# Row scatters cut into 18 and 28 pieces, each held back to TensorE's pace

## The chip, the cores and the metric

The kernel runs on one core of one Trainium2 chip. A core has TensorE (PE, matrix products), VectorE (DVE), ScalarE (ACT), GpSimd (POOL) and SyncE (SP, which only starts transfers), and 16 DMA engines. Each engine takes its own instructions strictly in order; they meet through semaphores. The metric is device time in microseconds (us) of a whole execution: the median of 3 runs of the kernel before is 1061.18 us (1056.96 to 1062.02). Lower is better.

## The reference, cut to what matters

Two layers work on x of 16 x 256 tokens by 128 values. Layer 0 is gated linear attention and a mixture of 8 experts; layer 1 is causal attention with 16 heads and a mixture of 16 experts. In each, every token goes to its two best experts.

```python
x = L0_attn_x
xn = _layernorm(x)
s = _L0_attn_ref(xn, ...)            # linear attention in chunks of 64, a scan over chunks
g = _silu(_L0_ffn_ref(xn, ...))      # top 2 of 8 experts
x = x + s * g
xn = _layernorm(x)
s = _L1_attn_ref(xn, ...)            # softmax(q k^T / sqrt(8)), causal, 16 heads of 8
g = _silu(_L1_ffn_ref(xn, ...))      # top 2 of 16 experts, tanh * cos(softplus)
return x + s * g
```

The kernel computes only the chosen experts. For this it sorts token rows by expert: every row (its 128 values and one number that says where the result goes) is scattered twice, once for each chosen expert, to a table in device memory (`xs`). The expert stage then reads the table in groups of 512 rows.

## The kernel before, in words

All engines run the same walk (`walk`, L272) over named stages, and each does its own part of a stage. Three stretches matter here.

**Chunks.** `gla(t, part)` is one third of a step of the linear attention. A step t holds work of several batch elements at once: the gates of element t, the decays, queries, keys and values of t-1, the scores of t-2, the states and outputs of t-3, and the normed output of t-4. On GpSimd a step has two small operations: `output_gates(t-4)` in part 0 (a product of 128x256, L1721, from step 4 on), for which DVE's `gated` (L1417) waits, and `chunk_ends(t-1)` in part 1 (a copy of 128x12, L1715), which waits for ACT's exponential (L896). The steps t = 1 to 6 come after `route(0)`, which computes the row numbers, and before the first expert stage. The scan of `decays` on DVE (L1366) marks the steps in a trace.

**The first scatter.** `scatter(0, i, n)` issues 64 indirect transfers from GpSimd (L1685), each of 128 rows, in n pieces. One piece of 6 stands ahead of each of the steps 1 to 6. Then SP loads the first rows of the table (`begin`, `rows`), for which it waits until all 64 have landed, and TensorE turns them (`turn`, L550). TensorE's `turn(0, 0)` stands behind step 6.

**The second attention and the second scatter.** `mha(a, b)` runs eighths a to b-1 of the second attention: each batch element has 8, of which the first six compute scores (`mha1`: L672 to L702) and the last two weigh and turn values (`mha2`: L714, L649). Eighths 32 to 59 run after `route(1)`, four ahead of each `mf(t)`, and beside them stands the second scatter, 64 transfers in 7 pieces. `mf(c)` loads and splits an eighth of the expert weights (ACT L863, DVE L1344); TensorE's first product with them (L586) waits for the last. `turn(1, 0)` again waits for rows that SP loads when all 64 transfers have landed.

GpSimd's transfers wait among themselves only (16 semaphores `rows_moved`, so at most 16 are under way, and every eighth one of the second half also waits for a small table of numbers, L1681). Nothing holds them to TensorE's pace, apart from where `output_gates` and `chunk_ends` stand between them.

Of the kernel before, what the change touches and what calls it, by code (L numbers as in the profile page):

```python
# [51 lines left out]
def build(nc, A, out):  # L52
    with ExitStack() as ctx:
# [7 lines left out]
        def sig(name, per=1):  # L61
            return Sig(ctx.enter_context(nc.semaphore(name)), per)
# [24 lines left out]
        thr, jj, part = cst[:, 664:728], cst[:, 728:808], cst[:, 936:937]  # L87
# [129 lines left out]
        gate2, gate2_ln, decay = sig("gate2", 2), sig("gate2_ln", 4), sig("decay", 3)  # L217
        pn, p_ends = sig("exp_decay", 2), sig("chunk_ends")
        qk, qk_mul = sig("qk", 4), sig("qk_scaled", 4)
        vv, v_moved = sig("v"), sig("v_moved", 2)  # L220
# [24 lines left out]
        m_s2, m_exp = sig("m_s2", 12), sig("m_exp", 12)  # L245
        m_pv, m_pv_act, m_pv_dve = sig("m_pv", 2), sig("m_pv_act"), sig("m_pv_dve")
        m_ot, m_y = sig("m_o_turned", 2), sig("m_y", 4)
# [4 lines left out]
        def last_scatter(l, i):  # L252
            return rows_moved[i].sem, 64 * l + 64
# [18 lines left out]
        def walk(do):  # L272

            def mha(a, b):

                for i in range(a, b):
                    if i % 8 < 6:
                        do["mha1"](i // 8, i % 8 // 2, i % 2 * 2)
                    else:
                        do["mha2"](i // 8, i % 2)  # L280
# [7 lines left out]
                    do["gla"](t, part)  # L288
            do["route"](0)
            for t in range(1, 7):  # L290
                do["scatter"](0, t - 1, 6)
                if t == 1:
                    do["set_later"]()
                for part in range(3):
                    do["gla"](t, part)
                for c in range(8 * (t - 1) // 6, 8 * t // 6):
                    do["w1"](c)
# [14 lines left out]
                    do["norm_end"](g - 2)  # L312
            do["route"](1)
            for t in range(7):
                do["scatter"](1, t, 7)
                mha(32 + 4 * t, 36 + 4 * t)
                do["mf"](t)
            do["mf"](7)
            do["ffn1_begin"]()
# [16 lines left out]
        def _(eng):  # L336
# [447 lines left out]
            def nothing(*_):  # L784
                pass
# [835 lines left out]
        def _(eng):  # L1621
# [39 lines left out]
            def route(l):  # L1661
                eng.wait_ge(*chosen[l].at(1))
                eng.memset(RS[l]["onesc"], 1.0).then_inc(routed_ones.sem, 1)

            def scatter(l, i, n):
                if i == 0:
                    if l == 0:
                        eng.wait_ge(*id_table.at(0))
                    else:
                        for j in range(16):  # L1670
                            eng.wait_ge(*last_scatter(0, j))
                    eng.tensor_copy(xid, idt[:, 0:32]).then_inc(ids_set.sem, 1)
                    eng.wait_ge(*routed[l].at(0, 14))
                    eng.wait_ge(zeroed[l].sem, 16 * (9 + l))
                    eng.wait_ge(*ids_set.at(l, 0))
                for m in range(64 * i // n, 64 * (i + 1) // n):
                    k, t = m // 32, m % 32
                    if k and t % 8 == 0:
                        for j in range(8):
                            eng.wait_ge(rows_moved[(t + j) % 16].sem, 64 * l + 16 * ((t + j) // 16 + 1))  # L1680
                        eng.tensor_copy(xid[:, t:t + 8], idt[:, 32 + t:40 + t]).then_inc(ids_set.sem, 1)  # L1681
                        eng.wait_ge(*ids_set.at(l, 1 + t // 8))
                    if m >= 16 or l:
                        eng.wait_ge(rows_moved[m % 16].sem, 64 * l + 16 * (m // 16))
                    eng.indirect_dma_start(xs[l][:, :], bass.IndirectOffsetOnAxis(ap=slot_i[l][:, m:m + 1], axis=0),  # L1685
                                           xrow[:, t, :], None).then_inc(rows_moved[m % 16].sem, 16)
# [260 lines left out]
```

## Time and profile before

| what | value |
|---|---|
| median of 3 runs | 1061.18 us |
| profiled execution, span from first to last instruction | 1209.8 us |
| mean granted TensorE clock in it | 0.820 |
| TensorE matmuls busy | 865.3 us (72%) |
| DVE, ACT, GpSimd busy | 644.2, 630.8, 461.6 us |
| GpSimd's row scatters (L1685), 128 of them | 126.6 us busy, 989 ns each |

The page gives no other time for the profiled execution than its span, so the span is taken as its own time. It is 148.6 us longer than the median of the runs without a profile. In the rows below a start is in us from the start of the span; "busy" leaves out waiting; in square brackets stands how long the engine sat idle before the row and what ended this. "another core or an unknown queue" and "remote" mean that the profile could not tell what released a wait; there is one core here. "issue" is time for which the profile shows no wait at all.

### The profile page before, as it was taken

Reading aid. Unit: us, or ns where it says so; the run is one execution under the profiler, and the core shown is the slowest. Engines: PE = TensorE matmul, PEld = TensorE weight load, DVE = VectorE, ACT = ScalarE, POOL = GpSimd, SP = SyncE. Lnnn points to the kernel's source line nnn. Section 1 sums busy time; section 2 is a strip of 40 time slices with the busy share of each in tenths; the row PEclk is TensorE's granted clock in tenths of the full one; section 3 lists DMA queues with packets and bytes.
Section 4 is the critical chain, followed back from the end, with each engine's and each line's share of the span. In section 5 each row is a group of like instructions: output and inputs, shape, how many; then the busy total and the mean of one; then the engine's idle time right before and its main releaser. Section 6 shows DMA issues by size and latency. Waiting matters only on the chain.

```text
span 1209.8 us, 23609 instructions
## 1 busy us (share of the span) xinstructions
PE 865.3 (72%) x8916; PEld 647.5 (54%) x8916; DVE 644.2 (53%) x1112; ACT 630.8 (52%) x1095; POOL 461.6 (38%) x486
## 2 busy tenths in 40 slices
PE   5735678989898987079773115989999999998510
PEld 3424566878787876055451003556766766666410
DVE  7663355655555422685575003766576566663345
ACT  5342356665756431255441003668788678876622
POOL 3075450213232344540004771004454455454635
PEclk9676778989898999576695556989999899998855
DMA  9411120000101120600003210210111011110052
GB/s 327 172 55 47 51 59 19 20 27 27 28 28 28 37 55 30 170 1 1 1 1 106 76 52 29 71 54 22 35 32 32 28 36 30 34 29 24 20 148 70
DMA packets 62366, 63.92 MB, mean 53 GB/s; under 512 B 7378, under 2 KB 52322, under 8 KB 62132
## 3 DMA queue, kind: packets, MB, share of 16 engines
q1 hardware_dynamic: 53300, 43.99, 12.5%
q0 software_dynamic: 8960, 18.43, 4.7%
q8 instruction: 77, 1.26, 0.5%
q14 instruction: 29, 0.24, 0.1%
HBM read 31.84 MB, written 30.55 MB: 52 GB/s over the span
## 4 chain that ended last, share of the span: by engine, by line
PE 41%; ACT 17%; issue 13%; DVE 13%; another core or an unknown queue 9%; POOL 4%; DMA 2%; SPq 0%; POOLq 0%; ACTq 0%; DVEq 0%
PE bank L434 4%; ACT L797 4%; PE bank L649 3%; PE bank L586 3%; PE bank L588 3%; POOL ys L1701 2%; PE bank L600 2%; PE bank L702 2%; PE bank L714 2%; PE bank L587 2%; ACT arena L1101 2%; PE bank L462 2%; PE bank L675 2%; PE bank L695 2%
## 5 line engine op out<-in xcount | busy, mean ns | idle before, releaser
L1701 POOL DMA_INDIRECT ys<-arena x152 | 152.4, 1003 | 192.6 <-DVE arena L1463 88.0
L1101 ACT ACTIVATE arena<-bank 128x512 f32<-128x512 f32 x192 | 101.6, 596 | 106.3 <-remote 50.2
L1571 DVE TENSOR_REDUCE arena<-bank 128x2 bf16<-128x512 f32 (+1 forms) x192 | 120.1, 682 | 67.4 <-issue 36.4
L1685 POOL DMA_INDIRECT xs<-arena x128 | 126.6, 989 | 62.2 <-issue 36.2
L586 PE MATMUL bank<-arena 128*128 128x128 bf16 x608 | 134.4, 228 | 11.3 <-DVE arena L1444 10.3
L588 PE MATMUL bank<-arena 128*128 128x128 bf16 x608 | 134.0, 228 | 0.7 <-issue 0.5
L587 PE MATMUL bank<-arena 128*128 128x128 bf16 x608 | 131.5, 223 | 1.1 <-issue 1.1
L797 ACT ACT_TABLE_LOAD x72 | 92.4, 1283 | 1.3
L434 PE MATMUL bank<-arena 128*128 128x256 f32 x256 | 72.0, 441 | 19.2 <-DVE arena L1350 15.8
L1741 POOL TENSOR_TENSOR arena<-arena 128x1024 f32<-128x1024 f32 x20 | 46.9, 2344 | 88.8 <-ACT arena L1016 88.8
L1453 DVE SCALAR_TENSOR_TENSOR arena<-arena,bank 128x512 f32<-128x512 f32 x36 | 24.7, 689 | 98.1 <-ACT arena L978 78.9
L586 PEld LDWEIGHTS bank<-arena 128*128 x608 | 61.0, 100 | 26.2 <-issue 14.4
L434 PEld LDWEIGHTS bank<-arena 128*128 128x128 f32 x256 | 55.7, 224 | 31.0 <-DVE arena L1350 16.9
L1491 DVE TENSOR_SCALAR arena<-bank 128x512 f32<-128x512 f32 x40 | 27.7, 692 | 81.6 <-ACT arena L1002 81.6
L649 PE MATMUL bank<-arena 128*128 128x256 f32 x256 | 68.6, 415 | 1.3 <-issue 1.0
L672 PE MATMUL bank<-arena 32*128 32x256 bf16 (+1 forms) x512 | 42.3, 261 | 37.0 <-issue 24.6
L1559 DVE SCALAR_TENSOR_TENSOR arena<-arena,bank 128x512 bf16<-128x512 bf16 x64 | 47.1, 746 | 34.4 <-ACT arena L1074 31.0
L590 PE MATMUL bank<-arena 128*128 x288 | 63.6, 221 | 0.0
L588 PEld LDWEIGHTS bank<-arena 128*128 x608 | 60.1, 99 | 6.2 <-issue 1.7
L587 PEld LDWEIGHTS bank<-arena 128*128 x608 | 61.2, 101 | 1.3 <-issue 0.8
L1074 ACT ACTIVATE arena<-bank 128x512 bf16<-128x512 f32 x64 | 37.6, 604 | 43.3 <-PE bank L649 42.4
L695 PE MATMUL bank<-arena 32*128 32x128 bf16 (+1 forms) x512 | 41.9, 266 | 25.3 <-issue 16.0
(213 smaller groups left out, 2116.4 us busy)
## 6 DMA issues: line engine op xcount, KB each, us to landing
xs<-arena SPq DMA_DIRECT2D x19, 516.0 KB, 8.1
arena<-xs SPq DMA_DIRECT2D x38, 258.0 KB, 2.8
arena<-ys SPq DMA_DIRECT2D x32, 256.0 KB, 5.2
arena<-in_MF SPq DMA_DIRECT2D x8, 512.0 KB
ys<-arena POOLq DMA_INDIRECT x152
arena<-in_x SPq DMA_DIRECT2D x8, 256.0 KB, 5.6
arena<-in_W SPq DMA_DIRECT2D x8, 256.0 KB, 2.9
xs<-arena POOLq DMA_INDIRECT x128
```

Of the source, the lines that this page charges most:

```text
L434: i = mm(k[:, 256 * h:256 * h + 256], (Wq, Wk)[n // 2][:, 128 * hh:128 * hh + 128], xnT[:, cols])
L586: mm(o, hi, b[:, 0, c4], stop=False)
L587: mm(o, hi, b[:, 1, c4], start=False, stop=False)
L588: i = mm(o, lo, b[:, 0, c4], start=False, stop=(l == 1))
L590: i = mm(o, b1r[:, 128 * c:128 * c + 128], b1s[:, bass.DynSlice(v * 128, 128)], start=False)
L649: j = mm(k[:, 256 * z:256 * z + 256], Wqk[:, c:c + 128], xnT[:, 256 * b:256 * b + 256])
L695: mm(k[:, w * m:w * m + w], K[p, g, q0:q0 + 128], Q[p, g, q0:256], start=(m == 0), stop=False)
L797: eng.preload_act_table_set(name)
L1101: act(PT[kt_][:, i, gs[0]:gs[0] + len(gs), :], bank_of["s2", b, n, i][:, :].rearrange("p (g q) -> p g q", q=w), ACT.Exp, scale=8 ** -0.5). ...
L1571: red(negM[b % 2][:, u, 32 * i + gs[0]:32 * i + gs[0] + len(gs)], kv_, op=ALU.max, negate=True).then_inc(m_max.sem, 1)
L1685: eng.indirect_dma_start(xs[l][:, :], bass.IndirectOffsetOnAxis(ap=slot_i[l][:, m:m + 1], axis=0), xrow[:, t, :], None).then_inc(rows_move ...
L1701: eng.indirect_dma_start(ys[l][:, :], bass.IndirectOffsetOnAxis(ap=yid[g % 4][:, j:j + 1], axis=0), y[:, 128 * j:128 * j + 128], None).the ...
```

## The change

The two scatters are cut finer and set between smaller parts of the other work: the first into 18 pieces, one ahead of each third of the steps 1 to 6, the second into 28, one ahead of each of the eighths 32 to 59. From the third piece on, GpSimd waits ahead of a piece until TensorE has done the part that stands beside the piece two before it. The total of 64 transfers per scatter, their data and their targets stay.

```diff
             for t in range(1, 7):
-                do["scatter"](0, t - 1, 6)
-                if t == 1:
-                    do["set_later"]()
                 for part in range(3):
+                    do["scatter"](0, 3 * (t - 1) + part, 18)
+                    if t == 1 and part == 0:
+                        do["set_later"]()
                     do["gla"](t, part)
...
             for t in range(7):
-                do["scatter"](1, t, 7)
-                mha(32 + 4 * t, 36 + 4 * t)
+                for e in range(4 * t, 4 * t + 4):
+                    do["scatter"](1, e, 28)
+                    mha(32 + e, 33 + e)
                 do["mf"](t)
...
+            def part_multiplied(k):
+
+                t = 1 + k // 3
+                return gate2.at(t) if k % 3 == 0 else vv.at(t - 1) if k % 3 == 1 else qk.at(t - 1)
+
+            def eighth_multiplied(i):
+
+                t, r = i // 8, i % 8
+                return m_s2.at(t - 1, 2 * r + 1) if r < 6 else m_pv.at(t - 1) if r == 6 else m_ot.at(t - 1)
+
             def scatter(l, i, n):
+                if i >= 2:
+                    eng.wait_ge(*(part_multiplied(i - 2) if l == 0 else eighth_multiplied(32 + i - 2)))
```

The semaphores that the new waits read are TensorE's: `gate2`, `v` and `qk` in the chunks, `m_s2`, `m_pv` and `m_o_turned` in the second attention.

On GpSimd the end of the first scatter, in step 6, stood like this before (128x256 is `output_gates(2)`, 128x12 is `chunk_ends(5)`, the two TENSOR_SCALAR belong to the stage behind):

```order
L1685 DMA xs<-arena 9216x129 [waits rows_moved12]
L1685 DMA xs<-arena 9216x129 [waits rows_moved13]
L1685 DMA xs<-arena 9216x129 [waits rows_moved14]
L1685 DMA xs<-arena 9216x129 [waits rows_moved15]
L1721 TENSOR_TENSOR arena<-arena 128x256 [waits o_rs]
L1715 COPY arena<-arena 128x12 [waits state,exp_decay]
L1640 TENSOR_SCALAR arena<-arena 128x256 [waits ld_ffn0]
```

And on GpSimd in the same step now (128x8 is the table of numbers):

```order
L1734 TENSOR_TENSOR arena<-arena 128x256 [waits o_rs]
L1694 COPY arena<-arena 128x8 [waits rows_moved12,rows_moved11,rows_moved13,rows_moved10,rows_moved14,rows_moved9,rows_moved15,rows_moved8,qk]
L1698 DMA xs<-arena 9216x129 [waits rows_moved8,ids_set]
L1698 DMA xs<-arena 9216x129 [waits rows_moved9]
L1698 DMA xs<-arena 9216x129 [waits rows_moved10]
L1698 DMA xs<-arena 9216x129 [waits rows_moved11]
L1728 COPY arena<-arena 128x12 [waits state,exp_decay]
L1698 DMA xs<-arena 9216x129 [waits rows_moved12,gate2]
L1698 DMA xs<-arena 9216x129 [waits rows_moved13]
L1698 DMA xs<-arena 9216x129 [waits rows_moved14]
L1698 DMA xs<-arena 9216x129 [waits rows_moved15]
L1641 TENSOR_SCALAR arena<-arena 128x256 [waits ld_ffn0]
```

The product and the copy have moved ahead of eight and of four of the last transfers, and the last four now stand behind an operation that waits for ACT.

The end of the second scatter on GpSimd before (the two copies of 128x4 open the second expert stage):

```order
L1685 DMA xs<-arena 10240x129 [waits rows_moved9]
L1685 DMA xs<-arena 10240x129 [waits rows_moved10]
L1685 DMA xs<-arena 10240x129 [waits rows_moved11]
L1685 DMA xs<-arena 10240x129 [waits rows_moved12]
L1685 DMA xs<-arena 10240x129 [waits rows_moved13]
L1685 DMA xs<-arena 10240x129 [waits rows_moved14]
L1685 DMA xs<-arena 10240x129 [waits rows_moved15]
L1694 COPY arena<-arena 128x4 [waits ld_rows0]
```

And now, with the waits for eighths 55 (`m_o_turned`), 56 and 57 (`m_s2`):

```order
L1698 DMA xs<-arena 10240x129 [waits rows_moved9,m_o_turned]
L1698 DMA xs<-arena 10240x129 [waits rows_moved10]
L1698 DMA xs<-arena 10240x129 [waits rows_moved11,m_s2]
L1698 DMA xs<-arena 10240x129 [waits rows_moved12]
L1698 DMA xs<-arena 10240x129 [waits rows_moved13,m_s2]
L1698 DMA xs<-arena 10240x129 [waits rows_moved14]
L1698 DMA xs<-arena 10240x129 [waits rows_moved15]
L1707 COPY arena<-arena 128x4 [waits ld_rows0]
```

Nothing has changed its place here but the waits: the last three transfers cannot start before TensorE has done eighth 57, behind which it has two eighths left.

## Rows read from the trace of the kernel before

**Rows 1.** All cores: span and mean granted clock.
```profile
core 0: 1209.8 us, clock 0.820
```
**Rows 2.** Chain of waits in order of time: start us, us, what.
```profile
92.56 14.10 another core or an unknown queue
114.80 11.45 another core or an unknown queue
137.95 11.78 another core or an unknown queue
...
657.87 7.88 another core or an unknown queue
668.24 26.93 issue
699.26 37.88 another core or an unknown queue
```
**Rows 3.** Stretches: length, each engine's busy us, clock, DMA share, GB/s.
```profile
668.00:696.00 28.00, 2.88 (x16) 1.67 (x18) 1.39 (x2) 0.84 (x2) 21.32 (x24) 0.50 0.17 54
...
762.00:782.00 20.00, 19.09 (x223) 11.60 (x224) 14.28 (x23) 12.63 (x25) 0.00 (x0) 1.00 0.18 54
```
**Rows 4.** Timeline of TensorE: start us, busy us, operation, idle before it.
```profile
653.23 0.28 PE L672 MATMUL bank<-arena 32*128 32x128 bf16 x1
...
723.85 0.26 PE L699 MATMUL bank<-arena 4*128 4x128 bf16 x1 [2.54 <-issue]
...
764.14 0.71 PE L658 MATMUL bank<-arena 128*128 128x128 f32 x4 [0.22 <-DVE arena L1571]
...
783.99 0.71 PE L658 MATMUL bank<-arena 128*128 128x128 f32 x4 [0.22 <-DVE arena L1571]
```
**Rows 5.** Timeline of GpSimd: first and a late transfer of each scatter.
```profile
61.00 1.28 POOL L1685 DMA_INDIRECT xs<-arena  x1 [12.21 <-DVE arena L1304]
...
102.86 0.96 POOL L1685 DMA_INDIRECT xs<-arena  x1 [0.30 <-issue]
...
648.91 1.53 POOL L1685 DMA_INDIRECT xs<-arena  x1 [12.06 <-DVE arena L1304]
...
730.17 0.96 POOL L1685 DMA_INDIRECT xs<-arena  x1 [0.30 <-issue]
```
**Rows 6.** Timeline of the chunks: DVE at steps 1, 2 and 6.
```profile
70.30 2.30 DVE L1366 TENSOR_TENSOR_SCAN arena<-arena 128x1024 f32<-128x1024 bf16 x1
...
80.44 2.29 DVE L1366 TENSOR_TENSOR_SCAN arena<-arena 128x1024 f32<-128x1024 bf16 x1
...
176.53 2.29 DVE L1366 TENSOR_TENSOR_SCAN arena<-arena 128x1024 f32<-128x1024 bf16 x1
...
183.47 0.49 DVE L1417 TENSOR_TENSOR arena<-bank,arena 128x128 f32<-128x128 f32 x2
...
191.25 0.69 DVE L1409 TENSOR_TENSOR arena<-bank,arena 128x512 f32<-128x512 f32 x1 [0.17 <-PE bank L434]
```
**Rows 7.** The same step: GpSimd's copy of chunk ends, TensorE's first turn.
```profile
180.87 0.20 POOL L1715 COPY arena<-arena 128x12 f32<-128x12 f32 x1 [1.53 <-ACT arena L896]
...
191.49 0.60 PE L550 MATMUL bank<-arena 128*128 128x128 f32 x4
```
**Rows 8.** Landing of an indirect transfer (chain) and of rows (page, issues).
```profile
489.31 2.23 DMA ys<-arena
...
arena<-xs SPq DMA_DIRECT2D x38, 258.0 KB, 2.8
```
**Rows 9.** End of the second attention: TensorE and ACT.
```profile
796.07 0.39 PE L702 MATMUL bank<-arena 128*128 128x256 bf16 x2
...
799.99 0.60 PE L550 MATMUL bank<-arena 128*128 128x128 f32 x4
...
802.76 0.61 ACT L969 ACTIVATE arena<-bank 128x512 bf16<-128x512 f32 x1
...
805.30 0.28 PE L586 MATMUL bank<-arena 128*128 128x128 bf16 x1 [4.71 <-DVE arena L1444]
```

## The prediction

> **What bounds the kernel now.** I read the spans first [rows 1]: the profiled execution took 1209.8 us, the runs without a profile 1061.18. A gap of 148.6 us has to be explained before any row is used, because a change can remove time that only the profiled execution has.
>
> The chain of waits in order of time shows where it may lie [rows 2]. Most steps of the chain are 1 to 5 us of real work; six long ones are waits with no cause that the profile knows: 14.1, 11.5 and 11.8 us beside the first scatter and 7.9, 26.9 and 37.9 us beside the second, 110 us in all. The stretches say what the engines do meanwhile [rows 3]: from 668 to 696 TensorE is busy for 2.9 us of 28, DVE for 1.4, ACT for 0.8, and only GpSimd works (21.3 us, 24 operations). The DMA engines are 17% busy, so it is not bandwidth. From 762 to 782, the same attention with no scatter beside it, TensorE is busy 19.1 us of 20. And in the timeline single small matmuls with no semaphore between them stand over 2 us apart ("2.54 <-issue") [rows 4]: TensorE isn't waiting for a result, it is kept from issuing. GpSimd itself is not slowed: its transfers start 1.27 us apart throughout.
>
> Two readings. Either a stream of indirect transfers stalls the other engines in every execution, or it does so only while all of it is being recorded. The 110 us fit into the 148.6 that only the profiled execution has; if the runs had the stalls too, 148.6 us of other recording cost would have to hide elsewhere, and I find no idle stretches of that size. I take it that the runs have few or none. The Trainium skill ("NOTIFIC — the notification-queue block", 7.1, overflow) says that this block's internal pipeline always pushes back on its producers rather than lose a record, which would permit such a stall in a profiled execution only; its section 10 also says a record costs an engine no cycles, which would put the stalls into the runs as well. No row here decides; the sum below uses the gap alone.
>
> **The kernel without the stalls.** So both stretches have to be laid out again, by rows from undisturbed places.
>
> First scatter: step 1 to step 2 took 10.1 us from scan to scan, step 6 took 15.4 (176.53 to the end of L1409 at 191.94) [rows 6]. For step 3 I estimate 12, for step 4 14. The scans of steps 1 to 6 then stand at 70.3, 80.4, 92.4, 106.4, 121.8 and 137.2, and the first turn 15.0 behind the last (191.49 - 176.53) at 152.2 [rows 6, 7]. GpSimd needs 1.34 us per transfer: the 32 of them from 61.00 to 103.82 took 42.8 us with two small copies between [rows 5]. In step 4 the product `output_gates(0)` stands behind 42 transfers (64*4/6), so it starts at 61 + 42*1.34 = 117.3. DVE wants it 6.9 us behind its scan (183.47 - 176.53) [rows 6], so with some 1.2 us for the product itself it should start at 112.1. DVE waits 5.2 us, and its gate work for the next step is queued behind that wait. At step 5 GpSimd starts the product at 133.5 against 132.7 wanted, at step 6 it is even. So the turn comes at 152.2 + 5.2 + 0.8 = 158.2. In the profiled execution this doesn't show, since the stalled TensorE lets GpSimd run ahead.
>
> Second scatter: GpSimd issues from 648.91 to 731.13, 64 transfers in 82.2 us [rows 5]. The attention starts its eighth 32 at 653.2; a batch element of 8 eighths takes 19.85 us (764.14 to 783.99) [rows 4], the last four take 7 (two take 799.99 - 796.46 = 3.5) [rows 9]. It would end at 653.2 + 59.6 + 7 = 719.8. The last transfer lands 2.2 us after its issue, the rows load in 2.8 [rows 8]: 736.2. So without stalls GpSimd is the later by 16 us, and the attention waits at its end.
>
> **The change, part by part.** It removes and adds no work: 128 transfers and the same products. It adds 42 waits.
>
> (a) Finer pieces beside the chunks. `output_gates(0)` now stands behind 10 pieces of 18, 35 transfers: 61 + 35*1.34 = 107.9, ahead of the 112.1 at which it is wanted; that of step 6 behind 56 instead of 64. DVE no longer waits: 6.0 us gone. What is late next is the scatter's own end: 64 transfers and a few copies, 61 + 85.8 + 1.5 = 148.3, then 2.2 and 2.8 and SP's 0.4 or so: 153.8 for the turn instead of 152.2. Gain 158.2 - 153.8 = 4.4 us. Queued behind each piece on GpSimd are only those products and copies, so a late piece would delay `gated` on DVE. The bounds: nothing gained if a transfer costs GpSimd 1.0 us without a profile (its busy time of 0.96 without the gap of 0.30 [rows 5]), since then 42 of them end at 105 and nobody waited; and 6 if the end of the scatter is hidden.
>
> (b) The waits beside the chunks. Piece 17 waits for TensorE's part 15, the first of step 6, and stands behind `chunk_ends(5)`, which waits for ACT. In the profile's step 6 this copy ends at 181.07; four transfers at 1.27, landing and load give 181.07 + 5.1 + 2.2 + 0.4 + 2.8 = 191.6 against a turn at 191.49 [rows 7, 8]: just hidden. I take 0; at most 2.4, if TensorE ran at its high clock there and so came earlier. The other waits are met, as TensorE is ahead of a GpSimd that is busy all the time.
>
> (c) The waits beside the attention. A piece is 2.29 transfers, 2.9 us; an eighth is 19.85/8 = 2.5 us. GpSimd is the slower and falls behind TensorE, so the waits bind at most at the start: pieces 0 and 1 are issued at about 654.5 and eighth 32 ends at about 655. Up to 1 us once, and it goes straight through, because the scatter's end is what counts: +1.0. If a transfer costs 1.0 us instead, 64 of them end at 713 and land and load by 718, the attention (719.8) is the bound, and the new wait for eighth 57 is exposed: from its end at 796.46 three transfers (3.8), 2.2, 0.4 and 2.8 give a turn at 805.7 instead of 799.99 [rows 8, 9]. Of these 5.7 us some 2.9 hide behind the last weight split, for ACT takes the turned rows only at 802.76 [rows 9]. From a turn at 805.7 to L586 is 0.6 + 0.6 + 0.7 and two hand-overs, 808.2 against 805.30: +3.
>
> (d) The 42 waits as such: no row shows an added wait of GpSimd's that is already met, bounds 0 and 0.1 us each by the shortest gaps in GpSimd's rows; most lie in the gap of 0.30 that each transfer has anyway. Taken as 0.
>
> The Trainium skill ("Perfetto Trace Analysis", DMA Instruction — SWDGE) says that such a row ends when the descriptors are written, not when the data has moved; by the trace 2.2 us follow [rows 8], and they are in the sums.
>
> Sum without stalls: -4.4 + 0 + 1.0 + 0 = -3.4 us. Against the median of the runs: 1061.2 - 3.4 = 1057.8, so 1058. Against the profiled execution's own time the stalls come in: at most three pieces, some 7 transfers, can be issued between two advances of TensorE, while the first long stall of the second scatter began after some 15 [rows 2, 5] and the groups of four in the expert stages show none of that size. I expect the profiled span to fall by 30 to 100 us, to 1110 to 1180, far more than the time.
>
> **Rivals.**
> 1. The runs have the stalls too, and pacing removes them. For it: the stalls are the profile's plainest feature and every engine but GpSimd shows them. Against it: the gap of 148.6. It would give, if half of the 110 us went, 1061 - 55 = 1006; if a tenth of the stalls is in the runs, 1061 - 11 - 3 = 1047.
> 2. Slower: the exposed tail. A transfer costs GpSimd 1.0 us without a profile, nobody waited for GpSimd before, and the waits chain the scatters' ends to TensorE's last parts. Price: 3.0 at the end of the attention, 2.4 at the end of the chunks, up to 1 for the waits: 1061.2 + 6.4 = 1067.6. It decides as soon as 64 transfers take less than 66 us (1.03 each). Against it: the 1.27 us stand at the same value in stalled and in free stretches, so it looks like GpSimd's own.
> 3. Nothing binds: the early products were not waited for (steps a little longer than my estimates of 12 and 14), GpSimd sets the end of the second scatter as before: 1061 to 1062.
>
> **Chances.** The forecast (a gain of 1 to 6 us) 0.45, rival 1 0.12, rival 2 in part or whole 0.21, rival 3 0.22. The forecast's own range is 1054 to 1061. The whole range runs from 1045, which holds the mild form of rival 1, to 1067. A measurement of this kernel can tell about 0.5%, 5.3 us, from no change. Faster than that (below 1055.9): all of rival 1 and a good third of the forecast, 0.30. Slower (above 1066.5): part of rival 2, 0.15. Within: 0.55.
>
> **What the changed profile would show.** (a) right: DVE's L1417 of steps 4 to 6 never waits for GpSimd's product, and the product follows its ACT releaser at once. (b) right: SP's first row load in the chunks at most 1 us ahead of where TensorE wants it. (c) right: the last transfer of the second scatter starts after eighth 57, within 4 us of its end. The stalls: stretches beside the second scatter with TensorE busy for more than half instead of a tenth, the chain without steps of 27 and 38 us, and the time nearly unchanged nevertheless. Wrong would be: a time below 1045 (the stalls were real), one above 1067 (more hangs on the scatters' ends than I see), or a profiled span that hardly falls (it isn't the length of the stream that stalls the others).

## The result and the profile after

| | before | after |
|---|---|---|
| median | 1061.87 us (13 executions, 1056.33 to 1067.55) | 1067.65 us (13 executions, 1063.9 to 1209.08) |
| ratio | | 1.0064, 95% interval 1.0039 to 1.009 |
| profiled execution: time, span, mean granted clock | no time on the page, 1209.8, 0.820 | 1068.76, 1066.9, 0.856 |

The change makes the kernel slower: the medians are 5.8 us apart, the ratio says 6.8 (0.64% of 1061.87). The forecast was 1058, a gain of 3.4, with a range of 1045 to 1067. Every ratio here leaves out executions more than 1.5% above the fastest of their kernel, so it can differ from the quotient of the medians beside it; of the changed kernel it leaves out one of 1209.08 us (mean granted clock 0.625), without which the median is 1066.8.

The span after stands beside a span before of 1209.8 [rows 1], but that is no pair: the new profile has none of the long stalls. A second profile of the unchanged kernel, taken for the experiments, has none either. It is the one to compare with. The spans of before (second profile) and after:

```profile
core 0: 1059.0 us, clock 0.856
```
```profile
core 0: 1066.9 us, clock 0.856
```

Both are 1.9 us below the time of their own execution (1060.93 and 1068.76), and these times lie among those of the other executions (1060.93 beside a median of 1061.14). So recording an execution does not by itself bring the stalls, and the gap of 148.6 us on which the prediction rested has another cause. It is found below.

**Where the 7 us are.** First GpSimd's timeline in the kernel after, at the start of the second scatter (start, busy, engine and line, idle before it and what ended it):

```profile
596.69 1.53 POOL L1698 DMA_INDIRECT xs<-arena  x1 [12.06 <-DVE arena L1305]
...
605.03 0.95 POOL L1698 DMA_INDIRECT xs<-arena  x1 [2.69 <-PE bank L703]
...
608.04 0.96 POOL L1698 DMA_INDIRECT xs<-arena  x1 [0.80 <-PE bank L703]
...
617.51 0.96 POOL L1698 DMA_INDIRECT xs<-arena  x1 [0.94 <-PE bank L703]
...
626.52 0.96 POOL L1698 DMA_INDIRECT xs<-arena  x1 [2.99 <-PE bank L717]
...
629.28 0.96 POOL L1698 DMA_INDIRECT xs<-arena  x1 [0.54 <-PE bank L728]
```

Five waits for TensorE, 8.0 us in all, 6.5 more than the five gaps of 0.30 that stand there otherwise. After 629 no gap ahead of a transfer that ends with TensorE is longer than the usual 0.30. TensorE meanwhile, by two stretches (length, busy time of PE, PEld, DVE, ACT, POOL with counts, granted clock, DMA share, GB/s):

```profile
596.00:630.00 34.00, 28.56 (x232) 16.05 (x232) 18.62 (x36) 12.91 (x24) 20.77 (x21) 0.62 0.42 148
630.00:677.00 47.00, 44.82 (x514) 26.48 (x510) 35.13 (x58) 29.38 (x55) 36.41 (x39) 1.00 0.37 107
```

The mean granted clock of the first stretch is 0.62. Taken by 5 us, it is 0.50 (the level of 1.2 GHz) from 580 to 620, 0.80 from 620 to 625 and 1.00 (2.4 GHz) behind. TensorE's rows show the pause ahead of it and the pace at either level:

```profile
600.75 0.68 PE L404 MATMUL bank<-arena 16*128 16x80 f32 x2 [15.37 <-issue]
601.02 0.28 PE L673 MATMUL bank<-arena 32*128 32x128 bf16 x1
...
619.21 1.03 PE L703 MATMUL bank<-arena 128*128 128x512 bf16 x2
...
629.69 0.40 PE L673 MATMUL bank<-arena 32*128 32x128 bf16 x8 [0.69 <-DVE arena L1560]
...
639.80 0.60 PE L703 MATMUL bank<-arena 128*128 128x512 bf16 x2
...
649.55 0.40 PE L673 MATMUL bank<-arena 32*128 32x128 bf16 x8 [0.69 <-DVE arena L1560]
```

The first batch element's eight eighths take 28.7 us (601.02 to 629.69), the second's 19.9 (629.69 to 649.55). The prediction took 19.85 us for the eight [rows 4], from a place at the high clock. The eighths are not alike either. The six that compute scores take 3.2 us each in the first element (to 620.24) and 1.8 in the second; the two behind them take 4.7 and 4.6. So the long wait of 2.99, for the products that weigh values (L717, eighth 38), is for one of the two long eighths, behind six slow ones, and the first wait of 2.69 also holds TensorE's late start: it begins eighth 32 at 601.02, 4.3 us behind the first transfer.

The chain of waits of the kernel after (start, length, what) shows that the last transfer sets when the expert stage starts:

```profile
687.12 2.51 DMA xs<-arena
...
689.77 2.78 DMA arena<-xs
692.55 0.14 issue
692.69 1.10 PE bank L551 x4
...
695.50 0.28 PE bank L587
```

TensorE at that place in the second profile of before, and in after:

```profile
685.30 1.08 PE L550 MATMUL bank<-arena 128*128 128x128 f32 x4 [9.57 <-DMA arena<-xs]
688.11 0.29 PE L586 MATMUL bank<-arena 128*128 128x128 bf16 x1 [1.73 <-DVE arena L1444]
```
```profile
692.69 1.08 PE L551 MATMUL bank<-arena 128*128 128x128 f32 x4 [16.05 <-DMA arena<-xs]
695.50 0.28 PE L587 MATMUL bank<-arena 128*128 128x128 bf16 x1 [1.73 <-DVE arena L1445]
```

TensorE sits idle for 16.05 us instead of 9.57. Counted from the scatter's first transfer (595.23 and 596.69), the turn comes after 90.1 us before and 96.0 after: 5.9 us of the loss.

**Beside the first scatter** the change gains almost nothing. DVE in the second profile of before (the product behind GpSimd's `output_gates`, steps 4 and 5) and in after, step 4:

```profile
118.52 0.49 DVE L1417 TENSOR_TENSOR arena<-bank,arena 128x128 f32<-128x128 f32 x2 [9.95 <-POOL arena L1721]
...
135.32 0.49 DVE L1417 TENSOR_TENSOR arena<-bank,arena 128x128 f32<-128x128 f32 x2 [0.77 <-POOL arena L1721]
```
```profile
114.05 0.49 DVE L1418 TENSOR_TENSOR arena<-bank,arena 128x128 f32<-128x128 f32 x2 [5.71 <-POOL arena L1734]
```

The wait of step 4 was there, and larger than predicted (9.95, not 5.2); the finer pieces take 4.2 us from it. But the turn moved only from 101.4 to 100.7 us behind the first transfer. It is now GpSimd's last transfer that sets it, as the prediction said of this end:

```profile
160.93 0.79 PE L551 MATMUL bank<-arena 128*128 128x128 f32 x4 [4.75 <-DMA arena<-xs]
```

### The profile page after: what moved, and what is told of

Its sections match the earlier page's. It is cut to its first block, busy times and chain, and to the rows that moved or that the text cites. A ratio compares the mean times of both kernels' runs of the same rounds, so it can differ in the third digit from the quotient of the medians.

```text
span 1066.9 us, 23643 instructions
## 1 busy us (share of the span) xinstructions
PE 818.5 (77%) x8915; PEld 620.0 (58%) x8916; DVE 644.3 (60%) x1112; ACT 630.1 (59%) x1095; POOL 467.3 (44%) x486
## 3 DMA queue, kind: packets, MB, share of 16 engines
q8 instruction: 77, 1.26, 0.5%
## 4 chain that ended last, share of the span: by engine, by line
PE 33%; issue 24%; POOL 18%; DVE 11%; ACT 9%; DMA 3%; SPq 1%; POOLq 0%; ACTq 0%; DVEq 0%
POOL xs L1698 8%; POOL ys L1714 7%; PE bank L650 5%; PE bank L587 3%; PE bank L703 3%; PE bank L715 3%; PE bank L676 2%; PE bank L673 2%; PE bank L696 2%; PE bank L615 2%; ACT L798 2%; PE bank L589 2%; PE bank L588 1%; PE bank L700 1%; DVE arena L1509 1%
## 5 line engine op out<-in xcount | busy, mean ns | idle before, releaser
L1698 POOL DMA_INDIRECT xs<-arena x128 | 133.3, 1041 | 67.8 <-issue 32.7
L587 PE MATMUL bank<-arena 128*128 128x128 bf16 x608 | 131.9, 227 | 4.6 <-DVE arena L1445 4.0
L589 PE MATMUL bank<-arena 128*128 128x128 bf16 x608 | 132.0, 227 | 0.0
L588 PE MATMUL bank<-arena 128*128 128x128 bf16 x608 | 129.3, 222 | 0.0
L1102 ACT ACTIVATE arena<-bank 128x512 f32<-128x512 f32 x192 | 101.5, 596 | 37.5 <-PE bank L703 37.5
L435 PE MATMUL bank<-arena 128*128 128x256 f32 x256 | 68.7, 428 | 15.5 <-DVE arena L1351 15.5
L435 PEld LDWEIGHTS bank<-arena 128*128 128x128 f32 x256 | 54.3, 218 | 25.0 <-DVE arena L1351 16.1
L650 PE MATMUL bank<-arena 128*128 128x256 f32 x256 | 67.7, 411 | 1.1 <-issue 0.7
L650 PEld LDWEIGHTS bank<-arena 128*128 128x128 f32 x256 | 49.8, 205 | 11.1 <-issue 3.9
L979 ACT ACTIVATE arena<-bank 128x512 f32<-128x512 f32 x36 | 21.6, 599 | 52.0 <-PE bank L591 51.9
```

What stands on the lines that cost most here:

```text
L435: i = mm(k[:, 256 * h:256 * h + 256], (Wq, Wk)[n // 2][:, 128 * hh:128 * hh + 128], xnT[:, cols])
L587: mm(o, hi, b[:, 0, c4], stop=False)
L588: mm(o, hi, b[:, 1, c4], start=False, stop=False)
L589: i = mm(o, lo, b[:, 0, c4], start=False, stop=(l == 1))
L650: j = mm(k[:, 256 * z:256 * z + 256], Wqk[:, c:c + 128], xnT[:, 256 * b:256 * b + 256])
L1102: act(PT[kt_][:, i, gs[0]:gs[0] + len(gs), :], bank_of["s2", b, n, i][:, :].rearrange("p (g q) -> p g q", q=w), ACT.Exp, scale=8 ** -0.5). ...
```

## The experiments

Four chips took part in the experiments. On two of them the kernel before takes 1061 to 1062 us, on the other two 1225 to 1228; each ratio is against the kernel before on the same chip. The chip of the given profile is not on record.

**1. The kernel before again, and the waits one scatter at a time** (before: 1061.14 us). The kernel before:

> The kernel before, unchanged, for a profile without the long stalls and as a measure of the comparison's own spread: ratio 1.000. The theory (both scatters end later than the attention beside them, so GpSimd's time from the first transfer to the last sets both stretches) expects in its profile a second scatter of 82 to 84 us from first to last transfer, TensorE idle 8 us or more ahead of the first turn of the second expert stage, and DVE's L1417 of step 4 waiting about 12 us for GpSimd's product. The rival (the attention sets the end, the waits expose a tail behind eighth 57) expects the last transfer ahead of the end of the attention and no idle time ahead of that turn.

Measured: 1060.93 us, the profile used above. No stretch of it has the stalls of [rows 2, 3]. The second scatter takes 84.7 us (82 to 84 expected), TensorE is idle for 9.57 us ahead of the turn, and DVE waits 9.95 us, not 12.

Without any wait (both lines gone):

```diff
-                if i >= 2:
-                    eng.wait_ge(*(part_multiplied(i - 2) if l == 0 else eighth_multiplied(32 + i - 2)))
```

> The changed kernel with its finer pieces and without all 42 waits. Theory: the waits cost some 7 us at the second scatter (its five longest waits are 2.7, 0.8, 0.9, 3.0 and 0.5 us) and nothing at the first, and the finer pieces gain 1 to 5 us at the first scatter: 1057 to 1061, ratio to the kernel before 0.995 to 1.000. Rival (the finer pieces themselves cost, since they put transfers beside other work that slows them): the time stays at 1066 to 1068.

Waits at the first scatter only:

```diff
-                if i >= 2:
-                    eng.wait_ge(*(part_multiplied(i - 2) if l == 0 else eighth_multiplied(32 + i - 2)))
+                if i >= 2 and l == 0:
+                    eng.wait_ge(*part_multiplied(i - 2))
```

> The changed kernel with the waits at the first scatter only. Theory: they are all met, so the time is that of the kernel without waits, 1057 to 1061, within 1 us of it. Rival (waits at the first scatter cost): 3 us or more above the kernel without waits.

At the second only (the line with the wait again without its other half):

```diff
-                if i >= 2:
+                if i >= 2 and l == 1:
```

> The changed kernel with the waits at the second scatter only. Theory: they are the whole of the loss, so the time is that of the changed kernel, 1066 to 1068, some 7 us above the kernel without waits, and the second scatter takes 90 to 92 us from first to last transfer. Rival (waits at the second scatter hidden): the time of the kernel without waits.

| | median us | ratio | 95% | second scatter, first to last transfer us |
|---|---|---|---|---|
| before | 1061.14 | 1 | | 84.7 |
| no waits | 1058.52 | 0.9988 | 0.9969 to 1.0008 | 85.3 |
| first only | 1061.0 | 1.0005 | 0.9989 to 1.0022 | 85.3 |
| second only | 1069.16 | 1.0095 | 1.0068 to 1.0121 | 90.3 |

The loss is in the 26 waits at the second scatter. The finer pieces alone change nothing that can be measured, nor do the waits at the first scatter: their median is 2.5 us above that without waits, more than the 1 us expected, but the intervals overlap, and in the profile no transfer of the first scatter waits for TensorE beyond the usual gap.

Why the pieces alone don't gain shows in TensorE and GpSimd of the version without waits:

```profile
159.03 1.08 PE L551 MATMUL bank<-arena 128*128 128x128 f32 x4 [6.45 <-DMA arena<-xs]
```
```profile
71.04 0.20 POOL L1726 COPY arena<-arena 128x12 f32<-128x12 f32 x1 [3.77 <-ACT arena L897]
...
153.42 0.97 POOL L1696 DMA_INDIRECT xs<-arena  x1 [0.30 <-issue]
```

and in GpSimd of the kernel before (second profile):

```profile
58.46 1.28 POOL L1685 DMA_INDIRECT xs<-arena  x1 [12.42 <-DVE arena L1304]
...
150.50 0.97 POOL L1685 DMA_INDIRECT xs<-arena  x1 [0.30 <-issue]
```

With 6 pieces the last transfer starts 92.0 us behind the first, with 18 pieces 95.1 (153.42 - 58.31): in step 1 the copy of chunk ends now comes after 7 transfers instead of 10, too early, and GpSimd waits 3.77 us for ACT, where before it did not wait at all. So DVE's gain is largely given back at the scatter's end. This is read from the two profiles; no version moved the copy back.

**2. A looser wait, a longer scatter, and filling the idle time** (before: 1061.11 us). The second scatter's pieces wait eight pieces back:

```diff
-                if i >= 2:
-                    eng.wait_ge(*(part_multiplied(i - 2) if l == 0 else eighth_multiplied(32 + i - 2)))
+                if i >= 8 and l == 1:
+                    eng.wait_ge(*eighth_multiplied(32 + i - 8))
```

> The fine pieces in both scatters; no waits at the first; at the second each piece from the ninth on waits for the eighth part of the attention eight pieces back instead of two (20 waits). Theory A (the loss of the change is that the pieces meet slow eighths at the start of the attention, where 28.7 us pass for the first eight of them): eight pieces back, piece 8 comes due 23 us after piece 0, eighth 32 ended after 10, and no wait binds. The time is that of the version without waits, 1058 to 1061, ratio 0.996 to 1.001, and the first to the last transfer take 85 us instead of 90. Theory B (a wait as such costs GpSimd some 0.2 us even when met, or any tie to TensorE does): 20 waits leave 4 us or more, 1063 to 1067.

Measured: 1059.56, ratio 0.9992 (0.9972 to 1.0012), first to last transfer 85.4 us. Theory A: a wait that doesn't bind costs nothing that can be seen.

No waits, and the second scatter issues eight of its transfers again at its end, which the load of the rows then also waits for (`last_scatter`, not shown):

```diff
+                if l == 1 and i == 27:
+                    for m in range(64, 72):
+                        eng.wait_ge(rows_moved[m % 16].sem, 64 + 16 * (m // 16))
+                        eng.indirect_dma_start(...)          # rows of transfer m - 24
```

> The fine pieces without any waits, but the second scatter issues eight transfers again at its end (72 instead of 64; the same rows to the same places). Theory A (the second expert stage starts when the scatter has ended, so each us of GpSimd there is one of the time): 8 transfers of 1.27 = 10.2 us later last transfer, turn and end, 1067 to 1070, ratio to before 1.006 to 1.010. Theory B (what follows has slack, since TensorE is short of work elsewhere too): a loss of under 5 us, 1059 to 1063.

Measured: 1071.67, ratio 1.0098 (1.0063 to 1.0132); first to last transfer 94.7 us, 9.4 more, and the time 11 to 13 us more than without them (1058.52 and 1059.32 in two measurements). So what is added to this scatter's end counts in full.

No waits, and two eighths of the attention taken out of the second expert stage and put into TensorE's idle time ahead of it:

```diff
+            mha(60, 62)
             do["mf"](7)
             do["ffn1_begin"]()
-            done, left = 60, 84
+            done, left = 62, 82
```

> The fine pieces without waits; eighths 60 and 61 of the second attention are taken out of the second expert stage and put ahead of it, where TensorE is idle for 11 us while the last rows land and load. Theory A (the idle time ahead of the turn is bound by the scatter alone): the two eighths fill 5 to 7 of the 11 us, the turn stays where it is, and the expert stage has 5 us less of attention in it: 1051 to 1055, ratio 0.990 to 0.995. Theory B (the expert stage is not bound by TensorE's or ACT's total work, or the eighths hold up the turn): 1056 to 1060, ratio 0.996 to 1.0.

Measured: 1080.97, ratio 1.02 (1.0164 to 1.0236). A miss of both theories. The turn did not come later (684.85, and 683.80 without the move), and TensorE's idle time ahead of it fell from 11.1 to 8.4 us, but the stage behind became slower. A stretch of 100 us in it, without and with the move:

```profile
750.00:850.00 100.00, 98.57 (x1151) 72.29 (x1152) 69.89 (x106) 88.40 (x139) 57.41 (x53) 0.98 0.13 37
```
```profile
750.00:850.00 100.00, 96.94 (x1070) 67.64 (x1069) 64.59 (x100) 82.61 (x130) 51.02 (x48) 1.00 0.12 33
```

TensorE gets through 1070 matmuls instead of 1151, at no lower clock. Other eighths now stand beside each third of an expert group; that this pairing is what costs is the likely reading, but no run shows it.

The same, and a third of step 7 of the chunks put ahead of the first expert stage, the later thirds moved up by one:

```diff
+            do["gla"](7, 0)
             do["ffn0_begin"]()
...
-                    if 7 + g < 20:
-                        do["gla"](7 + g, part)
+                    k = 22 + 3 * g + part
+                    if k < 60:
+                        do["gla"](k // 3, k % 3)
```

> As the version with eighths 60 and 61 moved ahead, and the same at the first stretch: the first third of step 7 of the chunks is put ahead of the first expert stage, where TensorE is idle for 6.5 us, and all later thirds move up by one. Theory A (that idle time is bound by the scatter alone): 3 to 5 us less than the version with the second stretch filled, 1047 to 1051. Theory B (the third of a step is longer than the gap, or the first expert stage is bound by a chain of waits): no change against it or 2 us more.

Measured: 1112.45, ratio 1.0496 (1.0464 to 1.0528): another 31 us lost, against both theories again. The thirds of the chunks now stand beside other thirds of the first expert stage too; what of this costs was not taken apart.

**3. Which of the 26 waits binds.** Waits at the third to eleventh piece of the second scatter only; only from the twelfth on; and four eighths put ahead of the stage instead of two, without waits. The edits, against the version with waits at the second only (the first two) and the one with two eighths ahead:

```diff
-                if i >= 2 and l == 1:
+                if 2 <= i < 11 and l == 1:
```
```diff
-                if i >= 2 and l == 1:
+                if i >= 11 and l == 1:
```
```diff
-            mha(60, 62)
+            mha(60, 64)
...
-            done, left = 62, 82
+            done, left = 64, 80
```

> The fine pieces in both scatters, no waits at the first; at the second only the third to the eleventh piece wait (9 waits, two pieces back), the 17 later ones don't. Theory A (the loss arises in the first batch element of this attention, whose eighths take 3.5 us at the low clock while a piece takes 2.9): the whole loss is here, 1066 to 1070, ratio 1.005 to 1.011, first to last transfer 89 to 91 us. Theory B (the loss is spread over all 26 waits): a third of it, 1060 to 1063.

> The counterpart: only the pieces from the twelfth on wait, two pieces back (17 waits). Theory A: TensorE is at its high clock by then, an eighth takes 2.5 us and a piece 2.9, so GpSimd is always the later and no wait binds: the time without waits, 1057 to 1061, first to last transfer 85 us. Theory B: two thirds of the loss, 1063 to 1066.

> The fine pieces without waits; four eighths (60 to 63) are put ahead of the second expert stage instead of two. Theory A (two eighths cost 20 us because each group of the stage then had other thirds of the attention beside its matmuls, while four, a whole group's worth, keep the pairing): the group takes 15.6 us again, the four fill the idle 11 us, and the stage has one group less with attention beside it: 1052 to 1060. Theory B (whatever work is put ahead of the stage starts it worse, by more transfers and loads late or a longer start): above 1066.

These ran on a chip on which the kernel before takes 1224.75 us (1214.95 to 1230.85, no execution below). Measured: early waits 1186.36, ratio 0.969 (0.9641 to 0.9739); late waits 1175.3, ratio 0.9559 (0.9509 to 0.9609); four eighths 1211.1, ratio 0.9899 (0.9853 to 0.9945). None of the expectations speaks of such a chip. Two things follow: the stalls of [rows 2, 3] are in all executions there, and on such a chip some of the waits gain 3 to 4%.

**4. The same questions again, with the whole change.** This fell on a chip without stalls (before: 1062.2 us).

> The whole change again, unedited. On a chip where the kernel before takes about 1061 us: 1067 to 1070, ratio 1.005 to 1.009, first to last transfer of the second scatter 90 us. On a chip where it takes about 1225 us because TensorE stalls beside the scatters: theory A (the waits break the stream of transfers up and so shorten the stalls): 1150 to 1185, ratio 0.94 to 0.97; theory B (the finer pieces alone do it): the same as the version without waits.

> The fine pieces without any wait, unedited against the earlier run. On a chip without stalls: 1057 to 1061. On a chip with them: theory A: 1210 to 1230, since nothing holds GpSimd back; theory B: as the whole change, 1150 to 1185.

> Waits only at the third to the eleventh piece of the second scatter. On a chip without stalls, theory A (the loss sits in the slow first eighths): 1066 to 1070; theory B (it is spread): 1060 to 1063. On a chip with stalls: as measured there, a ratio of 0.969.

> Waits only from the twelfth piece of the second scatter on. On a chip without stalls, theory A: no wait binds, 1057 to 1061; theory B: 1063 to 1066. On a chip with stalls: as measured there, a ratio of 0.956.

| | median us | ratio | 95% | first to last transfer us |
|---|---|---|---|---|
| whole change | 1066.52 | 1.0041 | 1.0023 to 1.0058 | 90.2 |
| no waits | 1059.32 | 0.9985 | 0.9965 to 1.0006 | 84.7 |
| early waits | 1066.62 | 1.0051 | 1.0028 to 1.0073 | 90.5 |
| late waits | 1065.29 | 1.0022 | 1.0 to 1.0045 | 86.7 |

(One execution of the whole change took 3965.33 us; it is in the median, which stays 1066.52 without it, and not in the ratio.) The whole change, at 1.0041, comes out a little below the 1.005 to 1.009 expected. The early waits alone bring the whole of the scatter's extra length and the whole loss, as theory A has it. But the late ones are not free, and there theory A is wrong: it expected 1057 to 1061, and the 1065.29 lies where theory B, a spread loss, put it. Yet a spread loss is not what it is either, since early and late losses add up to more than that of the whole change. The first of the late waits binds. GpSimd in the version with late waits:

```profile
632.85 0.96 POOL L1698 DMA_INDIRECT xs<-arena  x1 [4.45 <-PE bank L703]
```

By then GpSimd has run ahead through the whole slow start, and the first wait that stands there makes it pay for the lead. After it no wait binds. This accounts for part of the loss only: the scatter is 2.0 us longer than without waits and the turn comes 2.2 us later behind its first transfer (92.2 and 90.0), while the medians are 6 apart. The rest was not located.

**5. On a chip with stalls: the waits or the pieces?** (before: 1227.74 us, 1210.53 to 1237.28)

> The whole change, unedited. On a chip without stalls as measured twice: ratio 1.004 to 1.007. On a chip with them: theory A (waits break up the stream): ratio 0.94 to 0.97; theory B (the finer pieces do it): the same as j2.

> The fine pieces without waits. On a chip without stalls: ratio 0.997 to 1.001. On a chip with them: theory A: 0.985 to 1.005, theory B: as j1. The version with four eighths put ahead of the stage, which also has fine pieces and no waits, gave 0.990 there, which speaks for A.

> Fine pieces, no waits, eighths 60 to 63 ahead of the second expert stage. On a chip without stalls, theory A (the pairing of the attention's eighths with the expert groups is kept, the idle time is filled): 1052 to 1060. Theory B (work put ahead of the stage harms whatever its amount): above 1066. On a chip with stalls: as there, 0.990.

Measured: whole change 1156.03 (1149.13 to 1162.19), ratio 0.9468 (0.9401 to 0.9535); no waits 1224.61, ratio 0.9892 (0.9779 to 1.0005, from two of its six executions; the medians are 0.3% apart); four eighths 1219.62, ratio 0.9908 (0.9849 to 0.9967). Theory A: it is the waits, but for about 1% that the finer pieces may give. The kernel without them in the second scatter, by stretches:

```profile
648.80:680.00 31.20, 12.84 (x79) 5.31 (x79) 8.47 (x18) 2.78 (x6) 23.95 (x24) 0.50 0.43 150
680.00:722.00 42.00, 2.28 (x10) 1.12 (x10) 0.82 (x2) 1.19 (x2) 32.27 (x37) 0.50 0.16 52
722.00:760.00 38.00, 22.09 (x204) 12.86 (x206) 14.42 (x24) 12.21 (x23) 7.06 (x8) 0.67 0.13 42
760.00:806.00 46.00, 39.55 (x458) 24.32 (x454) 32.66 (x51) 30.27 (x54) 0.38 (x2) 0.99 0.22 64
```

For 42 us, in which GpSimd issues, TensorE gets 10 matmuls done (in before it is much the same [rows 3]). The last transfer is issued at 730.24, and TensorE runs steadily again from 740 on. With the waits:

```profile
627.00:660.00 33.00, 28.47 (x224) 15.81 (x224) 16.72 (x30) 12.09 (x24) 20.57 (x20) 0.62 0.42 151
660.00:700.00 40.00, 31.82 (x322) 18.01 (x321) 22.11 (x37) 17.29 (x32) 26.70 (x28) 0.87 0.27 83
700.00:729.00 29.00, 22.76 (x199) 13.02 (x198) 14.46 (x23) 12.63 (x23) 19.30 (x20) 0.76 0.25 77
```

No stretch like that is left, and TensorE is still not as busy as without stalls. From the second scatter's first transfer to the first product of the expert stage before took 156.4 us (648.91 to 805.30 [rows 5, 9]), the version without waits 157.3 (648.82 to 806.08), the whole change 110.6 (627.01 to 737.64). From the first scatter's first transfer to its turn it is 130.5 before [rows 5, 7], 124.2 without waits and 120.3 with the whole change. The two profiles of this chip, without waits and with them, have spans 75.2 us apart (1225.1 and 1149.9). Of these 46.7 lie beside the second scatter and 3.9 beside the first, 11.6 between the first turn and the second scatter, and 6.7 behind the first product of the second expert stage. Another 6.3 lie ahead of the first transfer (64.61 and 58.32), where the waits can't reach; what makes these last three was not followed up. The four eighths ahead of the stage could be measured only on chips with stalls, both times at 0.99. That is no worse than without waits alone (0.9892), so the 20 us that two eighths cost do not show with four there; whether they fill the idle time on one without stays open.

## Why the prediction was wrong, step by step

**What the spans' gap meant: wrong.** I took the stalls for something that only the given profile's recording brings. The runs show otherwise: profiled executions without stalls exist (1060.93 us, span 1059.0), and on two of four chips the kernel before takes 1210 us or more in every execution. The given profile was of an execution with stalls, the given times were of executions without. So the sum was made for the right case, which was luck: the reason was wrong. The sentence of the Trainium skill ("NOTIFIC — the notification-queue block", 7.1) that I weighed for a stall by recording has nothing in these runs that speaks for it. Its section 10, by which a record costs an engine no cycles, was not tested: every execution of the experiments has a span and a clock on record, with stalls and without (always 1.8 to 2.1 us below its time), and none was made without recording.

**(a) The finer pieces, -4.4: the term was mis-sized, measured -0.7** (101.4 to 100.7 us). DVE's wait at step 4 was there and got shorter, though it was 9.95 us and not 5.2, and 5.71 of it are left where I expected none. What failed is the end of the scatter, which I put at 64 transfers of 1.34 us whatever the pieces. That average came from steps 1 and 2 and holds two transfers of 1.83 us beside DVE's scans (so "1.27 us apart throughout" was misread); in the later steps such a transfer takes up to 2.87 (last section). The scatter takes 95.1 us between first and last transfer, not some 87, and 3.1 us more than with coarse pieces, because the copy of chunk ends, moved ahead of three transfers, waits for ACT. An estimate from these rows: with a last transfer at 92.0 us and the turn 5.6 us behind it, as here, the turn would come at 97.6 instead of 101.4, a gain of 3.8, close to the 4.4.

**(b) Waits beside the chunks, 0: right.** Without them 1058.52, with them 1061.0, and the intervals of the ratios overlap; first transfer to turn 100.7 and 99.7.

**(c) Waits beside the attention, +1.0: the step that failed.** "A piece is 2.29 transfers, 2.9 us; an eighth is 19.85/8 = 2.5 us. GpSimd is the slower": true from 630 us on, and false in the 29 us before, where an eighth takes 3.6 on average (28.7/8) at a mean granted clock of 0.62 (596 to 630). That is where the waits stand that bind. Measured: 5.9 us between the profiles of before and after, 5.7 and 4.8 between those with and without these waits, and 7.2 and 10.6 by the medians (1066.52 against 1059.32; 1069.16 against 1058.52), of which 1.5 and 5.9 were not located. The same misreading made the attention too short: I had TensorE done 16 us ahead of the turn, and without the waits it is 9.6 to 11.1. The second half of the step, that it goes straight through because the scatter's end counts, held: eight more transfers cost at least their full length.

**(d) The 42 waits as such, 0: right.** Eight pieces back, the waits cost nothing (0.9992 against 0.9988 and 0.9985).

The sum by the measured terms: -0.7 + 0 + 5.9 + 0 = +5.2, against +5.8 of the medians (the ratio's interval is +4.1 to +9.6).

**The signs.** A time above 1067 was named as a sign of being wrong, and it came. DVE still waits at step 4 (5.71 us), and TensorE waits 4.75 us for its first rows, which were to be loaded just in time; neither matches what was named for (a) and (b). The last transfer of the second scatter starts at 687.12, 14.2 us behind the end of eighth 57 (672.94), not within 4. The profiled span of 1110 to 1180 was forecast for an execution with stalls; the profile was of an execution without (1066.9), and where there are stalls it is 1149.9.

**Rivals.** Rival 2's price (1067.6) came out, its mechanism did not: a transfer costs 1.26 us (0.96 and 0.30) in every profile, and the tail of (c) isn't exposed. Rival 1 is true on the chips with stalls: 65 us by the ratio, 72 by the medians, more than the half of 110 I gave it. It needed executions that have them, and the times were of executions without. I had given it 0.12. None of the rivals was the one that came: waits that tie GpSimd too closely to TensorE while TensorE's clock is low.

## What to carry to other kernels

When a profile's span is far from the timed runs, don't put the difference down to recording: the two may be of different conditions, and a change may gain in one (here 5%) and lose in the other (0.6%). A wait that ties one engine to another's pace has to be costed at the slowest place of that pace, which here was just behind a pause, where TensorE's granted clock was 0.50; one that is only meant to keep the engines together should be looser than the lead that builds up there. Here eight pieces back cost nothing; whether so loose a wait still gains on a chip with stalls was not tried. And a wait of GpSimd's inside a stream that ends on the critical path costs its length even if nobody needed those transfers yet; where small operations are put between its transfers, place them behind the time at which their input is there (this last is read from the traces alone).

## What the runs showed of the hardware

- **There is a condition in which a stream of indirect transfers nearly stops the other engines.** On two of four chips it is in every execution (medians of 1225 and 1228 us against 1061). TensorE gets 10 matmuls done in 42 us at a DMA share of 0.16, and most of its idle time there has no releaser that the trace knows. Breaking the stream by waits for TensorE gave a ratio of 0.9468 (medians 72 us apart); cutting it finer without waits gave 0.9892, and the interval includes no change. What the condition is, and whether it belongs to the chip or to the time at which it was used, no run shows: each of the two chips was used once. The single execution of 1209.08 us is not known to be one of these: its clock was 0.625, where the same kernel has 0.835 to 0.858 in the condition.
- **GpSimd's issue of an indirect transfer is held while DVE scans.** In the second profile of the kernel before, a transfer that starts during the scan (GpSimd, then DVE):

```profile
126.67 0.98 POOL L1685 DMA_INDIRECT xs<-arena  x1 [0.28 <-POOL arena L1681]
127.96 2.75 POOL L1685 DMA_INDIRECT xs<-arena  x1 [0.30 <-issue]
```
```profile
127.65 2.29 DVE L1366 TENSOR_TENSOR_SCAN arena<-arena 128x1024 f32<-128x1024 bf16 x1
```

It ends at 130.71, 0.77 us behind the scan's end at 129.94, and takes 2.75 instead of 0.96. One transfer in each of the six steps does so (1.83, 1.83, 2.40, 2.43, 2.75, 2.87 us), 8.4 us in all. From first to last transfer, 63 steps of 1.26 us are 79.4, these holds make 88, and small copies, products and slightly longer transfers between them most of the rest of the 92.0 measured. A transfer that starts in the scan's first 0.03 us can go free: in the kernel after one at 79.66 takes 0.96, with the scan at 79.65. DVE's subtraction of two 128x1024 operands (L1345, of 1.2 us) holds a transfer in the same way (GpSimd, then DVE, in the kernel after):

```profile
630.54 1.94 POOL L1698 DMA_INDIRECT xs<-arena  x1 [0.30 <-issue]
```
```profile
630.44 1.21 DVE L1345 TENSOR_TENSOR arena<-arena 128x1024 bf16<-128x1024 f32 x1
```

The Trainium skill ("GPSIMD Engine Reference", Key points) says that GpSimd shares its memory interfaces with VectorE and contends with instructions of it that have two inputs in SBUF; these traces agree for both operations, whose two large inputs lie in SBUF.
